# Every tile that TensorE reads begins at a multiple of 128 bytes of its partition

## The reference, cut to what matters

```python
xn = layernorm(x)                        # x: 2048 tokens x 512
q, k, v = silu(xn @ Wq), silu(xn @ Wk), silu(xn @ Wv)    # 16 heads x 128
z, a, b = xn @ Wz, xn @ Wa, xn @ Wb
q, k, v = causal depthwise conv, 4 taps, of each
q, k = rope(q) / norm, rope(k) / norm
out = sum over lags s=0..3 of (q . k_s) * sigmoid(a_s * b) * scale * v_s   # k_s: k of s tokens ago
s = (out * rsqrt(mean(out^2) + eps) * norm_w * silu(z)) @ Wout
g = silu((relu((xn @ sign(up).T) * up_scale) @ sign(down).T) * down_scale * output_scale)
y = x + s * g
```

## The kernel before

| use | stationary | moving |
|---|---|---|
| project q, k, v, z (L768) | `whi_*`, `wlo_*`: 64 | `x_hi`, `x_lo`: 32 |
| up (L1218) | `up_sign`: 64 | `x_hi`, `x_lo`: 32 |
| down (L1233) | `hid_hi`, `hid_lo`: 96 | `down_sign`: 64 |
| output projection (L1248) | `hid_hi`, `hid_lo`: 96 | `x_hi`, `x_lo`: 32 |
| transposes (L826, L795) | `y_*`: 32 | `const`: 0 |
| scores (L894) | `rot_k`: 64 | `rot_q`: 32 |
| values (L810) | `v_tok`: 96 | `coef`: 96 (a block is 528 bytes) |
| gate selection in the preamble (L838, L839) | `const`: 0 | `v_tok`: 96 |

## Time and profile before

### The profile page before, as it was taken

How to read it: one execution, slowest core, us unless ns; L and a number is a source line. 1 busy time by engine, 2 the same in 40 slices (tenths; PEclk the granted TensorE clock), 3 DMA queues, 4 the chain that set the end, 5 groups by cost and what they waited for, 6 DMA issues and landing times. The chain is left out here.

```text
span 1431.2 us, 23209 instructions
## 1 busy us (share of the span) xinstructions
PE 1398.2 (98%) x7048; PEld 1166.4 (82%) x7048; DVE 1027.4 (72%) x1597; ACT 733.4 (51%) x2146; POOL 404.0 (28%) x504
## 2 busy tenths in 40 slices
PE   6999999999999999999999999997999999999998
PEld 4778888888888888888888888886788888788886
DVE  7889999999999999999989999995122222234442
ACT  5655655556655556565565665553554444332221
POOL 6152443434434344434443443422000000000001
PEclk9999999999999999999999999998899999999999
DMA  9123334433344233433334333333331101065454
GB/s 298 38 73 83 95 75 103 96 80 94 74 103 95 73 95 73 110 88 81 88 82 109 88 79 90 80 75 82 128 115 52 44 22 44 22 184 166 144 166 157
DMA packets 103962, 137.60 MB, mean 96 GB/s; under 512 B 11248, under 2 KB 48112, under 8 KB 103664
## 3 DMA queue, kind: packets, MB, share of 16 engines
q1 hardware_dynamic: 94704, 120.28, 29.4%
q0 software_dynamic: 9216, 16.78, 6.7%
HBM read 61.53 MB, written 25.17 MB: 61 GB/s over the span
## 5 line engine op out<-in xcount | busy, mean ns | idle before, releaser
L428 POOL TENSOR_TENSOR rnorm<-norms,neg_half 128x8 f32<-128x8 f32 x64 | 126.8, 1982 | 353.1 <-DVE norms L660 353.1
L635 DVE SCALAR_TENSOR_TENSOR y_k<-u_k,cw_k,y_k 128x512 f32<-128x512 f32 x192 | 159.6, 831 | 26.4 <-ACT y_k L533 18.1
L635 DVE SCALAR_TENSOR_TENSOR y_v<-u_v,cw_v,y_v 128x512 f32<-128x512 f32 x192 | 172.7, 899 | 6.9
L553 ACT ACTIVATE bank<-bank 128x128 f32<-128x128 f32 x512 | 133.6, 261 | 85.7 <-PE bank L826 85.7
L1137 DVE TENSOR_TENSOR hid_lo<-relu,hid_hi 128x512 fp32r<-128x512 f32 x64 | 44.3, 692 | 179.0 <-ACT hid_hi L1083 179.0
L635 DVE SCALAR_TENSOR_TENSOR y_q<-u_q,cw_q,y_q 128x512 f32<-128x512 f32 x192 | 144.4, 752 | 31.6 <-ACT y_q L533 23.5
L1055 POOL TENSOR_TENSOR g_buf<-g_buf,up_raw 128x512 f32<-128x512 f32 x3 | 3.8, 1282 | 411.0 <-DVE g_buf L1158 411.0
L1178 DVE TENSOR_TENSOR hid_lo<-o_raw,hid_hi 128x512 fp32r<-128x512 f32 x64 | 44.3, 692 | 102.9 <-ACT hid_hi L1103 102.9
L1079 ACT ACTIVATE relu<-bank,us_sb 128x512 f32<-128x512 f32 x64 | 44.0, 688 | 127.9 <-PE bank L1218 127.9
L1103 ACT ACTIVATE hid_hi<-o_raw 128x512 fp32r<-128x512 f32 x64 | 40.4, 632 | 123.5 <-PE bank L1248 120.8
L1233 PE MATMUL bank<-down_sign,hid_hi 128*128 128x512 f32 x256 | 101.4, 396 | 0.3 <-DVE hid_lo L1137 0.3
(11 more groups left out here) (173 smaller groups left out, 3565.5 us busy)
## 6 DMA issues: line engine op xcount, KB each, us to landing
swapped_q<-y_q SPq DMA_DIRECT2D x128, 128.0 KB, 2.3
swapped_k<-y_k SPq DMA_DIRECT2D x128, 128.0 KB, 2.3
sq_sum<-out_sq POOLq DMA_DIRECT2D x64, 256.0 KB, 3.4
o_scratch<-o_buf SPq DMA_DIRECT2D x64, 256.0 KB, 2.5
o_raw<-o_scratch SPq DMA_DIRECT2D x64, 256.0 KB, 3.2
raw_q<-in_wq SPq DMA_DIRECT2D x16, 256.0 KB, 3.1
raw_k<-in_wk SPq DMA_DIRECT2D x16, 256.0 KB, 3.6
raw_v<-in_wv SPq DMA_DIRECT2D x16, 256.0 KB, 4.5
```

The source lines that it names most:

```text
L428: nc.gpsimd.tensor_tensor(rnorm[:, g1 % 2, :], norms[:, g1 % 2, :], neg_half[:, 0:2 * BC], ALU.pow).then_inc(root_done, 1)
L553: last = nc.scalar.activation(block_of, block_of, ACT.Square, accum_out=norms[:, g1 % 2, i * BC + b:i * BC + b + 1])
L635: nc.vector.scalar_tensor_tensor(y[n][:, g % 2, :], u[n][:, g % 2, i:i + CH], cw[n][:, bass.ds(h * TAPS + i, 1)], y[n][:, g % 2, :], ALU.m ...
```

## The change

Three paddings of 96 bytes are put in (`gap_x` before `x_hi`, `gap_w` before the split weights, `gap_f` at the start of the last part; none is read or written), and some tiles of `attention` and `ffn_and_output` are declared in another order. No instruction is added or removed, none changes its shape, and no wait changes.

```diff
         neg_half = sb("neg_half", [P, 2 * NB])
+        gap_x = sb("gap_x", [P, 24])
         x_hi = sb("x_hi", [P, KT, S], f32r)
...
             raw = {n: sb(f"raw_{n}", [P, KT, D], at=att) for n in "qkvz"}
+            gap_w = sb("gap_w", [P, 24], at=att)
             w_hi = {n: sb(f"whi_{n}", [P, KT, D], f32r, at=att) for n in "qkvz"}
...
         sin = sb("sin", [P, S], at=ctx)
+        y = {n: sb(f"y_{n}", [P, 2, CH], at=ctx) for n in "qkv"}
+        rot = {"k": sb("rot_k", [P, S], at=ctx)}
+        v_tok = sb("v_tok", [P, NB, D], at=ctx)
+        coef = sb("coef", [P, 2, BC, BW], at=ctx)
+        rot["q"] = sb("rot_q", [P, S + LAGS], at=ctx)
         u = {n: sb(f"u_{n}", [P, 2, CH + HALO], at=ctx) for n in "qkv"}
-        y = {n: sb(f"y_{n}", [P, 2, CH], at=ctx) for n in "qkv"}
         swapped = {n: sb(f"swapped_{n}", [P, 2, CH], at=ctx) for n in "qk"}
-        rot = {"q": sb("rot_q", [P, S + LAGS], at=ctx), "k": sb("rot_k", [P, S], at=ctx)}
...
-        coef = sb("coef", [P, 2, BC, BW], at=ctx)
-        v_tok = sb("v_tok", [P, NB, D], at=ctx)
...
+        gap_f = sb("gap_f", [P, 24], at=ctx)
         up_sign = sb("up_sign", [P, KT, FT * P], f32r, at=ctx)
         down_sign = sb("down_sign", [P, FT, HID], f32r, at=ctx)
-        scale_row = sb("scale_row", [P, HID], at=ctx)
-        out_scale = sb("out_scale", [P, 1], at=ctx)
-        relu = sb("relu", [P, 2, CH], at=ctx)
         hid_hi = sb("hid_hi", [P, 2, CH], f32r, at=ctx)
         hid_lo = sb("hid_lo", [P, 2, CH], f32r, at=ctx)
+        scale_row = sb("scale_row", [P, HID], at=ctx)
+        relu = sb("relu", [P, 2, CH], at=ctx)
+        out_scale = sb("out_scale", [P, 1], at=ctx)
```

## The result

The changed kernel takes 1412.92 us (median of 4 runs, 1412.59 to 1413.44) against 1431.83 (median of 4) for the kernel before: 0.987 of it, interval 0.9855 to 0.9881, so 19 us faster. The forecast was 1365 us: the sign was right, the gain of 66 us was more than three times too large.

A forecast was written before the change was run, and what follows sets the result against it. PE was taken as the bound, with DVE taking over in attention after the change. Gains of 40.3 (attention), 16.7 (up and down) and 9.4 us (output projection), 66.4 together off 1431.2, gave 1365 us; range 1353 to 1434.

The forecast's parts named there:

- What bounds the kernel: In attention PE waits for nobody, busy 58.83 of 58.83 us a head; its own instruction stream is the time.
- The pitch's floor: A 512-column f32r matmul should take 213.3 ns plus 3.3, 216.6 ns, leaving 12.3 to 16.9 ns unexplained.
- Step 2: Matmul loops: the 4 to 4.6 ns between loops follow moving less stationary remainder and go when it is 0 everywhere.
- Step 1: f32r matmuls: a misaligned moving operand needs a seventeenth 128-byte piece, costing 32 columns, 13.3 ns.
- relative place only: Rival for the matmul loops: step 2 without step 1, all pitches come to 228.9 ns, 1413 us; chance 0.10.
- Step 3: PE's gain from matmul counts: 3.24 us a head, 16.7 us in up and down, 9.4 in output projection; 78 us.
- Step 4: Attention: DVE becomes the bound at 56.2 us a head, so the gain there is 2.6 us a head, 40.3 us.
- The other operands: Transposes, scores and values have nothing to gain; new places of u_* and raw_* put at zero, 1 us a head either way.
- Nothing happens: Rival for all matmul loops: the excess is the price of changing weights wherever they lie, 1432 us; chance 0.23.
- The streams collide: Slower rival: weight reads and moving stream at the same remainder clash, another 4.6 ns a matmul, 1454 us; chance 0.12.

The follow-up runs named there:

- f3: The changed kernel without the x_lo terms of q and k, 8 matmuls instead of 12 in two of four projections: 1389.71 us in one run.
- e1: The changed kernel without gap_x, both other paddings kept, so every tile lies 96 bytes lower: 1411.57 us, ratio 0.9856.
- second probe: A program of matmuls alone in attention's order, one step per distance of 0 to 252 bytes by 4: a step took 14.320 us at 0, 15.006 at 156.
- the version at 120: The changed kernel with the eight split weight tiles in one tile, 120 bytes (modulo 256) above x_hi and x_lo: 1406.28 us, ratio 0.982.
- q and k at 216: The changed kernel with the eight split weight tiles in one tile, 216 bytes (modulo 256) above x_hi and x_lo: 1415.64 us, ratio 0.987.
- d2: The changed kernel without gap_x: x_hi and x_lo stay at remainder 32, all weights, hid and down_sign at 0: 1433.15 us, ratio 1.0006.

## Why the prediction was right or wrong, by its own steps

**What bounds the kernel** was right. In every version but f3, which has fewer matmuls, PE is busy for the whole of a head, and attention and the last part move with its pitch alone.

**The pitch's floor** is the term of the sum that was mis-sized, and it made the miss. I took 3.3 ns beyond the columns for an `f32r` matmul because plain float32 ones have them. Measured: `f32r` matmuls of 512 columns took 226.6 to 226.7 ns on average in the best steady groups and no less in any, 13.3 beyond the columns, and at 256 columns it is 13.3 too. Of the 12.3 to 16.9 ns of excess that I counted as gain, only 2.2 to 6.8 could go. With 226.7 in place of 216.6 PE's gain would have been 16 x 192 x 6.8 ns + 1024 x 6.2 ns + 768 x 2.2 ns = 29 us, too little to bring DVE in, and the forecast 1402 us; most of what is left to 1413 is the settling below. bf16 at 215.8 ns shows that the short remainder exists, but not for this type. "TensorE: Matmul & The Clock Gate" of the Trainium skill, section Back-to-back issue gap, gives N/2.4 + 2.5 ns, 215.8 ns for 512 columns; the run agrees for bf16, and that figure doesn't hold for `f32r`. (Step 2 says that the sums would be 4 us larger by it. That holds for PE's gain; the final sum, with DVE as the bound in attention, would have grown by 1792 x 0.8 ns, 1.4 us.)

**Step 1, the seventeenth piece,** is refuted. Its evidence was that 12.3 is near 13.3; but those 13.3 ns are the floor and are there with 16 pieces too (the changed kernel) and no larger with 17 (e1, all at 32).

**Step 2, the relative place,** was the right mechanism and the whole of the gain. I had seen it as the difference between the output projection and the rest. The rival "relative place only" gave 1413 us, and 1412.92 was measured, with 0.10 given to it. That the numbers meet is luck, for its working was off in both directions: it had all pitches at 228.9, while they came to 226.7 where settled, and in attention 0.72 us a head over 192 matmuls are 3.8 ns less than 233.5, so 229.7 on average; the rest down to 226.7 is lost in settling. The remainders by 128 that I used were too coarse: distances 0 and 128 differ (226.7 and 232.8), and what I took for one -32 was 160 in `project` and 32 in down. That a distance of 0 would be a good one was not worked out either: in the second probe 60 of the 64 distances have a dearer step.

**Settling** was in no step: the prediction takes the pitch as one number for a loop, whatever ran before. In the changed kernel it keeps 16 x (192 x 6.8 ns - 0.72 us) = 9.4 us of what attention could have gained; the version at 120 wins 6.8 us of it back.

**Step 3's counts** and the sum's bookkeeping held: the same counts with the measured pitches give 19.4 of 19.6 us.

**Step 4, DVE,** was right in mechanism and size (f3) but never came into play, since PE's head of 58.11 stays above 56.5.

**The other operands** cost nothing, as said: transposes at 110 ns, DVE's work 54.08 us a head.

**The rivals.** "Nothing happens" is right for the largest part, the 13.3 ns that stay. Its cause, the change of weights, is not shown: in the set with the same weights throughout they were still loaded for each matmul, and the pitch was 232.8. "The streams collide" had the place wrong: distance 0 is among the best, and such losses exist elsewhere (244.5 ns at 156). Its sum was too small as well: the output projection, from 228.9 to 238.1, would have lost 9.2 ns a matmul and not 4.6, another 3.5 us.

What stays open is why. That the pitch depends on the distance of the two operands and on how a group is entered points to the reading of the next weights beside the stream, but no run took the weights' reading away, and half the weight columns made it cheaper at distances 128 and 160 and dearer at 0. The Trainium skill, "TensorE: Matmul & The Clock Gate", section Step-by-step: what each phase is for, gives the stream and the weights two independent read ports of the on-chip memory; by that their places should not matter to each other, and the table above differs. Open too is what decides whether a group settles: q and k at 216 do in one step and not in the next.

## What to carry to other kernels

When PE is full, work out its pitch per matmul and compare it between loops of the same shape; a few ns of difference are worth a layout. What to look for is the stationary operand's address less the moving one's, here modulo 256 bytes, and not whether either begins at a multiple of 128 (both began at multiples of 32; at odd multiples of 16 other distances are the good ones). Try it in the kernel, since a probe finds the steady pitch but not the cost of getting there. And never take a floor from an instruction of another type: one short program of the very matmul would have shown 226.7 ns.

## What the runs showed of the hardware that I had not expected

- An `f32r` matmul with new weights carries 13.3 ns beyond its columns (226.7 for 512, 120.0 for 256), a bf16 one 2.5 (215.8 for 512), a plain float32 pass of 512 columns 429.2.
- With the distance of its operands its pitch goes from 226.7 to 244.5 ns, in steps of 4 bytes without an order that I can see. With the moving operand at an odd multiple of 16 bytes other distances are the good ones (0 has 230.0, 32 has 226.7).
- The pitch has a memory: after plain float32 matmuls, or after `f32r` ones at another distance (down in d2), the same operands take up to ten matmuls to settle at 226.7. At distance 216 they settle at once in some steps of one kernel and never in others, and at distance 144 both 226.7 and 233.5 ns were steady.
- Half the weight columns changed the pitch both ways: 229.1 for 232.8 at distance 128, 231.3 for 233.3 at 160, 230.0 for 226.6 at 0.
